# A layout change in an attention and expert kernel: the split query and key parts lie in memory in another order, and the stacks are loaded in nine transfers instead of twelve

## The reference

```python
scores = jnp.einsum('bhsd,bhjkd->bhsjk', q, kb) * SCALE
scores = jnp.where(diag_mask[None, None], -jnp.inf, scores)
w = jax.nn.softmax(scores.astype(jnp.float32), axis=-1)
w = w * include[None, None, :, :, None]
out = jnp.einsum('bhsjk,bhjkd->bhsd', w, vb)
norm = jnp.sum(w, axis=(-2, -1), keepdims=False)[..., None]
return out / (norm + 1e-06)
```

## Time and profile before

| | us |
|---|---|
| median of 3 runs | 515.2 (515.1 to 517.5) |
| span of the profiled execution | 514.7 |
| TensorE busy | 427.9 (83%) |
| VectorE busy | 321.2 (62%) |
| ScalarE busy | 180.3 (35%) |
| GpSimd busy | 165.4 (32%) |
| a batch in the loop, from the first scores of batch 4 to those of batch 5 | 55.8 |

### The profile page before, as it was taken

One profiled execution on the slowest core, in us unless ns is written; L12 is line 12 of the kernel. 1 busy time (PEld: TensorE's weight loads), 2 busy tenths in 40 slices (PEclk: granted clock), 3 DMA queues, 4 the chain that ended last, 5 costly groups with the idle time before them and its releaser, 6 DMA issues.

```text
span 514.7 us, 10761 instructions
## 1 busy us (share of the span) xinstructions
PE 427.9 (83%) x3616; PEld 396.0 (77%) x3616; DVE 321.2 (62%) x872; ACT 180.3 (35%) x409; POOL 165.4 (32%) x274
## 2 busy tenths in 40 slices
PE   1746399789959995999857997899959999998885
PEld 1734379688849985999757996799959999897775
DVE  4425379839737874688524875488728868656241
ACT  2521025514414342533432324433434344434140
POOL 5320501003704152324521155233523214317162
PEclk9985659969969998999977999799989999899898
DMA  7498943912960079003930039201960110010000
GB/s 184 134 115 172 80 136 90 106 41 81 129 88 3 0 149 114 18 2 104 116 60 3 1 119 105 54 3 46 143 69 2 42 32 3 1 32 10 22 0 22
DMA packets 44078, 33.84 MB, mean 66 GB/s; under 512 B 2981, under 2 KB 41893, under 8 KB 43837
## 3 DMA queue, kind: packets, MB, share of 16 engines
q1 hardware_dynamic: 44028, 33.18, 40.4%
HBM read 23.21 MB, written 9.96 MB: 64 GB/s over the span
## 4 chain that ended last, share of the span: by engine, by line
PE 62%; DMA 19%; SPq 7%; DVE 4%; issue 4%; POOL 2%; ACT 2%; POOLq 0%; DVEq 0%; ACTq 0%
PE X L772 30%; DMA KS<-parts_d 16%; PE PO L866 11%; SPq L419 7%; PE SA L827 3%; PE SB L850 3%; DMA parts_d<-parts 2%; PE X L795 2%; PE SA L830 1%; PE SA L829 1%; PE SA L828 1%; PE SB L853 1%; DMA raw<-wqkv 1%; PE SB L852 1%; PE SB L851 1%
## 5 line engine op out<-in xcount | busy, mean ns | idle before, releaser
L667 DVE TENSOR_REDUCE nmax<-SA 128x12 f32<-128x384 f32 x128 | 66.8, 554 | 73.8 <-PE SA L830 73.6
L866 PE MATMUL PO<-VB,PT 128*128 128x68 f32 x768 | 98.5, 280 | 0.0
L866 PEld LDWEIGHTS PO<-VB,PT 128*128 128x128 f32 x768 | 93.5, 197 | 3.0 <-issue 2.7
L600 POOL TENSOR_TENSOR hid<-gsil,ups 128x256 f32<-128x256 f32 x64 | 47.3, 742 | 123.5 <-DVE ups L756 121.4
L827 PE MATMUL SA<-KS,QS 96*128 96x256 bf16 x128 | 41.9, 328 | 50.3 <-DMA KS<-parts_d 48.9
L772 PE MATMUL X<-x_h,wgu_h 128*128 128x256 f32 x256 | 78.0, 305 | 0.7 <-ACT sbc L512 0.5
L772 PE MATMUL X<-x_l,wgu_h 128*128 128x256 f32 x256 | 73.2, 286 | 0.0
L772 PE MATMUL X<-x_h,wgu_l 128*128 128x256 f32 x256 | 72.9, 285 | 0.0
L491 ACT ACTIVATE PT<-SB 128x384 f32<-128x384 f32 x128 | 56.0, 489 | 47.4 <-PE SB L853 36.6
L606 POOL TENSOR_TENSOR hid_l<-hid,hid_h 128x256 fp32r<-128x256 f32 x64 | 46.4, 732 | 39.1 <-ACT hid_h L523 38.9
L827 PEld LDWEIGHTS SA<-KS,QS 96*128 96x128 bf16 x128 | 13.9, 108 | 57.7 <-issue 30.1
(11 more groups left out here) (118 smaller groups left out, 988.4 us busy)
## 6 DMA issues: line engine op xcount, KB each, us to landing
parts_d<-parts SPq DMA_DIRECT2D x16, 384.0 KB, 2.9
QS<-parts_d SPq DMA_DIRECT2D x48, 128.0 KB, 7.2
KS<-parts_d SPq DMA_DIRECT2D x48, 128.0 KB, 8.0
x_sb<-x SPq DMA_DIRECT2D x8, 256.0 KB, 11.0
raw<-wgu SPq DMA_DIRECT2D x8, 256.0 KB, 3.9
xres<-x SPq DMA_DIRECT2D x8, 256.0 KB, 2.8
out<-x SPq DMA_DIRECT2D x16, 128.0 KB, 1.8
max_d<-mt_sb SPq DMA_DIRECT2D x8, 192.0 KB, 10.0
```

The costliest lines, as they stand in the source:

```text
L600: nc.gpsimd.tensor_tensor(hid[k % 2][:, :], gsil[k % 2][:, :], ups[k % 2][:, :], ALU.mult)\
L667: nc.vector.tensor_reduce(nmax[:, 0:NC_, h], SA[h % 2][:, 0:SC] .rearrange("p (c s) -> p c s", s=BS), AX.X, ALU.max, negate=True)\
L866: last = pe.matmul(o[:, dst:dst + PW], PT[k % 2][:, n, src:src + P], v[:, t, 2 * k + n, :], start=True, stop=True)
```

## The change

In `parts_d` the order becomes tile, part, dimension, head within the tile, position, so that for one part and one dimension the 8 heads of a tile lie one behind the other, 4 KB. A row of a stack is then two runs of 4 KB, one for each tile. For that the columns of the query and key weights are permuted before the launch (`dims_first`): the partition of a tile is now dimension times 8 plus head. The parts store writes 6 pieces of 512 bytes per partition instead of 2 of 1.5 KB. The loads are listed in `STACK_LOADS` as stack (0 is QS, 1 is KS), first group of 16 rows, first part, number of groups: where a stack holds consecutive parts in consecutive rows, they go in one load, of 48, of 32 or of 16 rows. The semaphores count to 9 x 16 instead of 12 x 16. The lines move down by 3 or 4.

```diff
+STACK_LOADS = ((0, 0, 0, 3), (1, 0, 0, 1), (1, 1, 0, 1), (1, 2, 0, 1), (0, 3, 0, 2), (1, 3, 1, 1), (1, 4, 1, 1),
+               (0, 5, 0, 1), (1, 5, 2, 1))
...
-                        wait(sp, stack_loaded[b.parity], b.pairs(16 * 12))
+                        wait(sp, stack_loaded[b.parity], b.pairs(16 * len(STACK_LOADS)))
...
-                    sp.dma_start(parts_d[b.parity, n].rearrange("(t q) p s -> q t (p s)", q=P),
-                                 parts[:, n, :, :, :].rearrange("q t p s -> q t (p s)")).then_inc(parts_stored, 16)
+                    sp.dma_start(parts_d[b.parity, n].rearrange("t p d h s -> (d h) (t p) s"),
+                                 parts[:, n, :, :, :].rearrange("q t p s -> q (t p) s")).then_inc(parts_stored, 16)
...
-                    for r in range(len(Q_PART)):
-                        for n, stk, part in ((0, QS, Q_PART[r]), (1, KS, K_PART[r])):
-                            src = parts_d[b.parity, n, :, part, :].rearrange("(h d) s -> d h s", d=HD)
-                            sp.dma_start(stk[b.parity][HD * r:HD * (r + 1), :, :], src)\
-                                .then_inc(stack_loaded[b.parity], 16)
+                    for n, first, part, count in STACK_LOADS:
+                        src = parts_d[b.parity, n, :, part:part + count].rearrange("t p d h s -> (p d) t (h s)")
+                        dst = (QS, KS)[n][b.parity][HD * first:HD * (first + count), :, :].rearrange("r (t h) s -> r t (h s)", t=KT)
+                        sp.dma_start(dst, src).then_inc(stack_loaded[b.parity], 16)
...
-                        pe.wait_ge(stack_loaded[b.parity], b.pairs(16 * 12, 16 * 12))
+                        pe.wait_ge(stack_loaded[b.parity], b.pairs(16 * len(STACK_LOADS), 16 * len(STACK_LOADS)))
...
+    def dims_first(w):
+
+        return w.reshape(KT, NH // KT, HD, H).transpose(0, 2, 1, 3).reshape(H, H)
+
+    w_q, w_k, w_v = (np.asarray(w) for w in (L0_attn_Wq, L0_attn_Wk, L0_attn_Wv))
+    wqkv = np.concatenate([on_partitions(w) for w in (dims_first(w_q), dims_first(w_k), w_v)], 2)
...
-    args["parts_d"] = nc.dram_tensor("parts_d", (2, 2, H, NPART, S), BF16, kind="Internal").ap()
+    args["parts_d"] = nc.dram_tensor("parts_d", (2, 2, KT, NPART, HD, NH // KT, S), BF16, kind="Internal").ap()
```

More of the change, by code:

```diff
@@ L963, in on_partitions @@
         return w.T.reshape(KT, P, -1).transpose(1, 0, 2)
-    wqkv = np.concatenate([on_partitions(np.asarray(w)) for w in (L0_attn_Wq, L0_attn_Wk, L0_attn_Wv)], 2)
+    def dims_first(w):
+        return w.reshape(KT, NH // KT, HD, H).transpose(0, 2, 1, 3).reshape(H, H)
+    w_q, w_k, w_v = (np.asarray(w) for w in (L0_attn_Wq, L0_attn_Wk, L0_attn_Wv))
+    wqkv = np.concatenate([on_partitions(w) for w in (dims_first(w_q), dims_first(w_k), w_v)], 2)
     wgu = np.asarray(L0_ffn_expert_gate_up).reshape(NE, KT, P, NI, 2).transpose(2, 0, 1, 4, 3)
```

## The result

The changed kernel takes 480.6 us (median of 5, 475.6 to 481.9) against 515.2 us before (514.1 to 517.5). The ratio is 0.929, with a 95% interval of 0.925 to 0.933. The forecast was 482.1 us. The profiled execution of after is the fastest of its five: 475.6 us, with a mean granted clock of 0.942 where the other four had 0.928 to 0.936, so some 5 us of what its trace shows gained are not in the median.

The account below looks back on a forecast made before the run. TensorE was taken as the bound, held up by eight stack-load waits and the half clock behind them. Span 514.7 - 30.0 (loads) - 4.1 (clock) + 1.0 (store) = 481.6, plus 0.5 to the median: 482.1 us; range 449 to 500.

Parts of the forecast that it names:

- The bound and the eight waits: TensorE, busy 83% of the span, bounds; its first scores' stack-load waits (line 827), one per batch, total 48.9 us.
- The saving a load: Stack loads: nine turns instead of twelve, 1.25 us each, make a load 3.75 us shorter; eight batches give 30.0 us.
- I take 0: Stack loads: 4 KB runs instead of 512-byte pieces gain nothing; the other end was 10.5 us a load.
- the sign against its main step: Stack loads: narrow loads moving at well over 105 GB/s would show that the length of a run mattered.
- if a wide load takes one turn like a narrow one: Stack loads: a 48-row load takes 1.25 us like a 16-row one, needing 315 GB/s.
- The rival with ten turns: Stack loads: wide loads only partly faster, 2.5 us less a load, 20 us in all, 496.2 us; chance 0.20.
- The clock: TensorE's half clock behind the last six waits, 31.3 us: 4.1 us saved behind the third, nothing taken for the others.
- The third wait's term: Batch 2's wait for the stack shrinks to 0.24 us, so the clock stays up behind it: 4.1 us saved.
- dear end: Parts store: if its 512-byte pieces moved at 105 GB/s and held up the loads, 22.4 us more; store rival's chance 0.08.
- The 1.0 us for the fill: Parts store: four stores in the way of the first two stack loads in the fill add 1.0 us.
- The second scores keep their distance: TensorE's second scores need max_d, which comes earlier by the same 3.75 us, so their distance from the first stays.
- The longest rival (451 us): Stack loads: length was the limit or long runs overlap; load 6.5 us, all eight waits go, 450.7 us; chance 0.18.

Follow-up runs that it names:

- e1: The changed kernel with its 4 KB runs and parts store, but twelve loads of 16 neighbouring rows instead of nine: 499.1 us, ratio 0.963.
- e6: e1 with its twelve loads reordered Q0 Q1 Q4 Q5 K0 K1 K4 K5 Q2 Q3 K2 K3: 485.0 us, ratio 0.938.
- e5: e1 with its twelve loads reordered by row groups 0, 2, 1, 3, 4, 5, query and key of each: 507.7 us, ratio 0.983.
- e3: The kernel before with one line changed: each of twelve loads fills every sixth of the 96 rows instead of 16 neighbouring ones; 456.5 us, ratio 0.882.
- e4: e1 with each of its twelve loads filling every sixth of the 96 rows instead of 16 neighbouring ones: 456.9 us, ratio 0.883.
- e7: The changed kernel with its nine loads and 4 KB runs dealt out on every second row: 456.0 us, ratio 0.883.
- e2: The changed kernel's nine loads with 512-byte pieces, rows in memory padded to 768 bytes, each parts store issued in two halves: 505.8 us, ratio 0.976.
- e8: The kernel before, 512-byte pieces and neighbouring rows, with its twelve loads issued in e6's order: 507.0 us, ratio 0.984.

## Why the prediction was right, and where it was wrong

**The bound and the eight waits: right.** The time came out of the wait at line 827 and of the clock behind it, and of nothing else. The forecast let 18.9 us of it stand, 15.8 us did.

**The saving a load: right in size, wrong in its parts, so the number is in part luck.** I took 3.75 us, and 16.8 - 13.0 = 3.8 us was measured. But I gave all of it to width and none to length. By e1 the length is worth 1.8 us, and the step from e1 to the changed kernel, the nine loads in their order, 15.0 - 13.0 = 2.0 us. Two steps failed. The first is "I take 0" for the longer runs. I held 6.1 against 6.6 GB/s per row, and neither number was the rate that I took it for. The 105 GB/s hold the borders, without which the stack's rows have 97 / 16 = 6.1 (109 / 16 = 6.8 with 4 KB runs); and in the stretch with the 24-row load the engines were busy for 0.48 only the earlier trace rows, so that 146 GB/s is not what these rows can take. In the stretch of narrow loads the changed kernel has 134 GB/s, what the prediction named as the sign against its main step; e6 has 132 with 4 KB runs and changing ways, so length and borders account for it. The prediction cites a rule of the Trainium skill ("DMA: Bandwidth & Descriptors", section "Specifications") by which pieces of 512 bytes are long enough, so that longer runs would be worth nothing; here the measurement decides against it, with 97 against 109 GB/s on one way. The second failed step is "if a wide load takes one turn like a narrow one": it needed 315 GB/s, and the stretch in which the 48-row load runs has 227, about twice the 109 of one way. Its three groups of rows lie on two ways by the theory of shared ways, so it takes two turns.

```profile
164.70:166.20 1.50, 1.50 (x15) 1.50 (x15) 0.61 (x2) 0.00 (x0) 1.25 (x3) 1.00 1.14 227
166.20:170.00 3.80, 3.80 (x30) 3.17 (x30) 3.09 (x9) 2.52 (x6) 2.49 (x4) 1.00 1.03 134
```

The rival with ten turns had the width's term nearer to the truth: 2.5 us, against the 2.0 us of the nine loads behind e1. The Trainium skill's "Door 1" section of "SBUF — State Buffer", cited there, is borne out: 227 GB/s is near its eight ports (about 218). Also e5's 109 GB/s across groups 1 and 3 fits its table, in which these rows have their ports in common. An estimate from these rows: ten turns of 128 KB at 109 GB/s are 12.0 us, less the 1.4 us that five borders gave and with 2.0 us for start and landing 12.6 us, against 13.0 measured. The forecast came out because the length that it left out was as large as the width that it counted too high. How much of the 2.0 us is width and how much the new order is open; with twelve narrow loads the order of e6 gave 0.7 us.

**The clock: mis-sized in the profiled execution.** The third wait's term was right: behind batch 2 the clock stays at 1.00. For the others I took nothing. Of the five stretches behind the later waits only two are still at 0.50 (126.2 and 228.6), behind waits of 3.81 and 2.00 us; behind 1.55, 1.28 and 1.16 us it stays up.

```profile
80.00:112.00 32.00, 30.17 (x290) 27.30 (x289) 27.96 (x76) 15.42 (x35) 6.97 (x12) 1.00 0.46 93
126.20:129.50 3.30, 3.30 (x21) 3.08 (x19) 3.23 (x10) 0.85 (x2) 0.73 (x1) 0.50 0.22 60
176.80:180.80 4.00, 4.00 (x39) 3.90 (x40) 2.71 (x6) 1.64 (x3) 1.42 (x2) 1.00 0.23 67
228.60:231.90 3.30, 3.30 (x19) 3.08 (x18) 1.75 (x4) 0.00 (x0) 1.32 (x2) 0.50 0.20 48
289.00:293.00 4.00, 3.94 (x39) 3.85 (x40) 2.71 (x6) 1.59 (x4) 1.67 (x3) 1.00 0.26 84
339.70:343.70 4.00, 3.96 (x39) 3.86 (x40) 2.71 (x6) 1.71 (x4) 1.78 (x3) 1.00 0.19 52
```

The 31.3 us at half clock behind the last six waits have become 6.6 us, 12.4 us saved where I had 4.1. These 8.3 us account for the 8.0 us by which the profiled span, 473.6 us, lies under the sum's 481.6; the 3.1 us more that the waits gave came back elsewhere. The other executions ran at a lower mean clock, so the median has less of it; how much less, the times alone don't part from the rest.

**The store: its dear end did not come.** The page gives a median of 2.9 us to landing, as before, where I had 3.2. The 1.0 us for the fill was not measured by itself.

**"The second scores keep their distance": of the maxima, not of TensorE.** They now wait 2.1 us in all for the maxima. The maxima's load did not fall behind: it is issued 179.03 - 176.80 = 2.2 us behind batch 4's first scores, where before it was 206.98 - 204.49 = 2.5 us. TensorE became faster. Its products between the first and the second scores took 210.36 - 204.49 = 5.9 us with most of them at half clock, and now take 181.97 - 176.80 - 0.88 = 4.3 us. The three waits stand behind batches 4, 6 and 7, where the clock stayed at 1.00, and there is none behind 3 and 5, where it fell. So part of what the clock gives, the wait takes back. The row of before, then that of after:

```profile
210.36 0.28 PE L850 MATMUL SB<-QS,KS 120*128 120x256 bf16 x1
...
181.97 0.28 PE L853 MATMUL SB<-QS,KS 120*128 120x256 bf16 x1 [0.88 <-DMA QS<-max_d]
```

**The longest rival (451 us)** described a load that no wait sees. Its price was near, its cause not: e3, e4 and e7 reach 456 to 457 us by other rows, not by longer runs.

## What to carry to other kernels

Before making runs longer or transfers fewer, compare the rate of the slow transfer with that of another of the same piece size in the same trace; if pieces of that size move faster elsewhere, look at which partitions it reaches. Where the order of rows is free, as in a sum over partitions, deal each load out over all of them by a step: one line took 12% off the time here. A rate read from a stretch is an average: read finer stretches before taking it for the rate of one kind of transfer, for here 105 GB/s hid 97 and 132. And test two halves of a change apart, for a sum that comes out right can hide two terms that are wrong.

## What the runs showed that was not expected

- Issuing a load whose destination rows have a step (e3, e4, e7) takes 0.63 to 0.65 us from one issue to the next, against 0.47 to 0.49 with neighbouring rows, whether its runs are short or long. e2's loads on neighbouring rows with padded memory rows take 0.65 us as well.
- Loads on different groups of rows overlap at their borders, and with short pieces no less than with long ones: eleven borders take 2.1 us off a load of 4 KB runs (e6, 14.4 to 12.3 us of data) and 2.6 us off one of 512-byte pieces (e8, 16.2 to 13.6 us). Most of it comes with the first five (1.4 us in e1 and in the kernel before).
- The granted clock fell behind waits of 2.0 and 3.8 us and not behind 1.2 to 1.6 us in the changed kernel, while before it fell after 1.04 us in several pieces.
